# Queries of two heads by seven products of parts instead of eight, in the two 32-head attentions of a four-layer decoder kernel

## The reference, cut to what matters

```python
q = (query @ wq).reshape(bs, sq, 32, 128).transpose(0, 2, 1, 3)
k = repeat(key @ wk, 4 heads of queries to a head of keys)
v = repeat(value @ wv, the same way)
q, k = rope(q), rope(k)            # x * cos + rotate_half(x) * sin
attn = softmax(q @ k.T / sqrt(128) + mask)
x = layernorm(x + (attn @ v) @ wo)
```

## Time and profile before

| | us |
|---|---|
| median of 3 runs (lowest, highest) | 2778.18 (2775.37, 2780.76) |
| the profiled execution, its own time | 2781.93 |
| its span, first to last instruction | 2780.6 |
| stage 1, first key product to last output product, about | 169 to 862 |
| stage 4, the same | 1146 to 1837 |

### The profile page before, as it was taken

One profiled execution on the slowest core, in us unless ns is written; L12 is line 12 of the kernel. 1 busy time (PEld: TensorE's weight loads), 2 busy tenths in 40 slices (PEclk: granted clock), 3 DMA queues, 4 the chain that ended last, 5 costly groups with the idle time before them and its releaser, 6 DMA issues.

```text
span 2780.6 us, 40315 instructions
## 1 busy us (share of the span) xinstructions
PE 2649.1 (95%) x15720; PEld 1751.7 (63%) x15720; DVE 1640.8 (59%) x3081; ACT 851.6 (31%) x2630; POOL 458.8 (17%) x511
## 2 busy tenths in 40 slices
PE   8989999999999799899999999999998899999998
PEld 7855666666655566556666666556774455666664
DVE  3556667666666555466676666654555644344455
ACT  0012232222233355222222222323444412333331
POOL 1022212222202100122122222122211121000002
PEclk9999999999999999999999999999999999999999
DMA  8530001110000100001001000010000010000000
GB/s 182 92 128 25 37 38 39 38 38 16 16 1 38 69 2 2 27 23 39 38 38 39 37 18 6 11 69 31 2 2 28 21 63 27 15 27 1 12 1 31
DMA packets 53819, 94.86 MB, mean 34 GB/s; under 512 B 29408, under 2 KB 38560, under 8 KB 47488
## 3 DMA queue, kind: packets, MB, share of 16 engines
q1 hardware_dynamic: 53632, 92.30, 10.6%
HBM read 83.89 MB, written 8.39 MB: 33 GB/s over the span
## 4 chain that ended last, share of the span: by engine, by line
PE 88%; DVE 7%; ACT 3%; issue 1%; POOL 0%; DMA 0%; DVEq 0%; SPq 0%; POOLq 0%; ACTq 0%
PE banks L628 19%; PE banks L666 12%; PE banks L620 4%; PE banks L687 4%; PE banks L303 3%; PE banks L710 3%; PE banks L1210 3%; PE banks L650 3%; PE banks L1720 3%; PE banks L1772 3%; PE banks L2010 2%; PE banks L2042 2%; PE banks L1749 2%; PE banks L2075 2%; PE banks L1725 2%; PE banks L697 2%
## 5 line engine op out<-in xcount | busy, mean ns | idle before, releaser
L628 PE MATMUL banks<-xT,weights 128*128 128x512 f32 x1024 | 458.2, 592 | 0.0
L748 ACT ACTIVATE E_x<-S_x,sm_x 128x128 f32<-128x128 f32 x512 | 199.3, 390 | 586.7 <-DVE sm_x L838 586.7
L628 PEld LDWEIGHTS banks<-xT,weights 128*128 128x128 f32 x1024 | 188.9, 190 | 209.5 <-issue 206.6
L888 POOL TENSOR_TENSOR QT<-QT,turned 128x512 f32<-128x512 f32 x128 | 162.4, 1268 | 708.1 <-DVE QT L781 506.4
L779 DVE TENSOR_TENSOR turned<-banks,const 64x512 f32<-64x512 f32 x160 | 109.5, 684 | 234.1 <-PE banks L628 233.6
L809 DVE TENSOR_TENSOR x<-banks,x 128x256 f32<-128x256 f32 (+1 forms) x312 | 159.1, 510 | 123.2 <-PE banks L666 117.6
L161 POOL TENSOR_TENSOR norm_spread<-norm_mv,const 128x1 f32<-128x1 f32 x96 | 20.9, 218 | 1205.0 <-DVE norm_mv L157 1205.0
L666 PE MATMUL banks<-weights 128*128 128x256 f32 x832 | 206.9, 381 | 0.0
L666 PEld LDWEIGHTS banks<-weights 128*128 128x128 f32 x832 | 151.8, 190 | 39.6 <-DVE x L809 12.1
L666 PE MATMUL banks<-weights,OT 128*128 128x256 f32 x624 | 165.1, 387 | 12.1 <-DVE x L809 10.8
L2138 ACT ACTIVATE E_s<-banks,top_s 128x128 f32<-128x128 f32 x512 | 139.3, 383 | 62.9 <-DVE top_s L2235 62.9
(11 more groups left out here) (294 smaller groups left out, 4578.0 us busy)
## 6 DMA issues: line engine op xcount, KB each, us to landing
weights<-in_L_xwq SPq DMA_DIRECT2D x16, 1024.0 KB, 4.8
weights<-in_L_xwo SPq DMA_DIRECT2D x16, 1024.0 KB, 7.3
weights<-in_L_xwk SPq DMA_DIRECT2D x16, 256.0 KB, 5.1
weights<-in_L_xwv SPq DMA_DIRECT2D x16, 256.0 KB, 5.4
weights<-in_L_ffn_W_base SPq DMA_DIRECT2D x3, 1024.0 KB, 4.9
weights<-in_L_xwq SPq DMA_DIRECT2D x4, 768.0 KB, 5.0
weights<-in_L_xwo SPq DMA_DIRECT2D x4, 768.0 KB, 5.7
xT<-in_xT SPq DMA_DIRECT2D x4, 512.0 KB, 9.8
```

What stands on the lines that cost most here:

```text
L628: mm = PE.matmul(bank[:, :], weight, source[:, k, half_of(i)], start=k == 0, stop=k == KC - 1)
L748: ins = AC.activation(e[:, j, :], s[:, j, :], ACT.Exp, bias=sm[:, 0, j:j + 1], scale=1.0, accum_out=sm[:, 1, j:j + 1])
L888: PO.tensor_tensor(dst, dst, turned[j % 2][:, :, :], ALU.add).then_inc(*x_roped.one())
```

## The change

**Queries.** The 8 query jobs of a group become 6, three for each pair of heads `p`. The matrix of weights of two heads and the matrix of x in two halves of tokens are both cut in four parts, and the four blocks of queries (C11, C12, C21, C22) come out of the 7 products P1 to P7, each of 2 products of 128x128 by 512 columns: P2 and P1 in a pair's first job, P5, P6 and P3 in its second, P4 and P7 in its third. P1, P6 and P7 add up in one bank, the rest passes through the bank beside it. ACT copies a block's other term out of that bank into QT (`OTHER`), then DVE adds the first bank to it (`add_queries`); the next job waits for that add.

**Sums of parts.** POOL makes four sums of parts of wq for each group (`wq_sums`, each 128x512). DVE makes eight of x once a stage (`sums_of_xT`). `wo_sums` and `ot_sums` write one of their sums in place; `ot_sums` has four operations still, each now waiting for the one before.

**Rotation.** Of queries, DVE makes only the two sine products, now from QT in SBUF (`turn_queries`), placed in the steps by `shares` right behind the normalising. POOL makes the cosine product and the addition, two operations in place of one. Keys are as before.

**Order.** `plans` holds 10 jobs (b0 two of keys, b1 two of queries, b2 one, b3 two, b4 one, b5 and b6 one of values each, b7 none). In the opening the jobs of the two pairs alternate, values follow the queries in banks 3 and 4, and the second pair has banks 5 and 6. wq, wk and wv have one buffer each. 24 pairs of units in place of 26 go by parts, so that 16 units are plain. S has two buffers, not three. Three later attentions share semaphores with one another.

```diff
-                plans = [(1, 2, 2, 2, 1, 1, 1, 0)] + [(2, 2, 2, 2, 2, 1, 1, 0)] * (G8 - 2)
+                JOBS = (("k", 0), ("k", 1)) + tuple(("q", n) for n in range(6)) + (("v", 0), ("v", 1))
+                QUERIES = (tuple(("q", n) for n in (0, 3, 1, 4, 2, 5)),) + (JOBS[2:8],) * (G8 - 1)
+                ADDED = {0: ("C11",), 1: ("C12",), 2: ("C21", "C22")}
+                OTHER = {0: ("C11",), 1: ("C22", "C12"), 2: ("C21",)}
+                plans = [(1, 1, 1, 1, 1, 1, 1, 1)] + [(2, 2, 1, 2, 1, 1, 1, 0)] * (G8 - 2)
+                shares = [(0, 1, 1, 1, 1, 2, 1, 1)] + [(0, 1, 1, 2, 1, 1, 1, 1)] * (G8 - 2)
-                pairs = (units - B) // 2 - 2
+                pairs = (units - 2 * B) // 2
...
+                        if turn == 0:
+                            product("P2").then_inc(*x_other.one())
+                            product("P1").then_inc(*x_query.one())
+                        elif turn == 1:
+                            product("P5").then_inc(*x_other.one())
+                            product("P6")
+                            PE.wait_ge(*x_other_here(8 * g + place_of(g, p, "C22", OTHER) + 1))
+                            product("P3").then_inc(*x_other.one())
+                        else:
+                            product("P4").then_inc(*x_other.one())
+                            product("P7").then_inc(*x_query.one())
...
+                    def turn_queries(g, m):
+                        DV.wait_ge(*x_qadd(8 * g + m + 1))
+                        sines(NR * g + 2 + m, query(g, *blocks_of(g, ADDED)[m])).then_inc(*x_taken.one())
...
-                        DV.tensor_tensor(OS[:, 0], a21, a22, ALU.add)
-                        then(DV.tensor_tensor(OS[:, 2], a11, a21, ALU.subtract))
-                        then(DV.tensor_tensor(OS[:, 1], OS[:, 0], a11, ALU.subtract))
-                        DV.tensor_tensor(OS[:, 3], a12, OS[:, 1], ALU.subtract).then_inc(*x_ot_sums.one())
+                        then(DV.tensor_tensor(OS[:, 1], a11, a21, ALU.subtract))
+                        then(DV.tensor_tensor(a21, a21, a22, ALU.add))
+                        then(DV.tensor_tensor(OS[:, 0], a21, a11, ALU.subtract))
+                        DV.tensor_tensor(OS[:, 2], a12, OS[:, 0], ALU.subtract).then_inc(*x_ot_sums.one())
...
+                    def rope(j, to, cosines):
+                        PO.wait_ge(*x_taken(j + 1))
+                        if cosines:
+                            PO.tensor_tensor(four(to), four(to), spread(cos128, 4), ALU.mult).then_inc(*pool_step.one())
+                            PO.wait_ge(*pool_step.all())
+                        PO.tensor_tensor(four(to), four(to), turned[j % 2][:, :, :], ALU.add).then_inc(*x_roped.one())
...
+                    wq_sums(0)
                     for g in range(G8):
-                        for i in range(NJ):
-                            if g and i == 7:
+                        for i in range(2):
+                            rope(NR * g + i, KT[g % 2][:, half_of(i)], False)
+                        for m in range(8):
+                            if m == 2 and 1 <= g and 8 * (g - 1) < 2 * pairs:
                                 wo_sums(g - 1)
+                            rope(NR * g + 2 + m, query(g, *blocks_of(g, ADDED)[m]), True)
+                        if g + 1 < G8:
+                            wq_sums(g + 1)
```

More of the change, by code:

```diff
@@ L497, in load_cross, with place_rest, quarter @@
                 SP.dma_start(ctxT[:, :, :], dram["ctxT"]).then_inc(*ctx_in.one())
[L499 to L505, removed]
+            used = 3621 if stage == 4 else 2600
+            rest, taken = arenas[1 - stage % 2], [used]
+            def place_rest(n):
+                taken[0] += n
+                return rest[:, taken[0] - n:taken[0]]
+            def quarter(t, k):
+                return t.rearrange("p (k n) -> p k n", k=k)
+            views = {name: quarter(a.place(P, KC * n), KC) for name, n in (("wq", D), ("wk", P), ("wv", P))}
+            views["wq_sums"] = a.place(P, 3 * D).rearrange("p (s k n) -> p s k n", s=3, k=2)
+            views["wo"] = [quarter(t, 4) for t in (a.place(P, 4 * D), place_rest(4 * D))]
+            views["wo_sums"] = place_rest(3 * D).rearrange("p (s k n) -> p s k n", s=3, k=2)
+            views["ot_sums"] = place_rest(3 * D // 2).rearrange("p (s k n) -> p s k n", s=3, k=2)
+            for name, here in (("wk", xwk_in), ("wv", xwv_in), ("wq", xwq_in)):
+                SP.dma_start(views[name], dram[f"{layer}_x{name}"][0]).then_inc(*here.one())
             SP.dma_start(views["wo"][0], dram[f"{layer}_xwo"][0]).then_inc(*xwo_in[0].one())
@@ L508, in load_cross @@
                 views["mask"] = a.load("mask")
+            views["xT_sums"] = [a.place(P, D) for _ in range(3)] + [place_rest(D) for _ in range(2)]
+            assert taken[0] <= rest.shape[1]
             return layer, views, a.here.all()
@@ L512, in cross @@
             norm = Norm((0, 1))
-            wo, WS, OS = views["wo"], views["wo_sums"], views["ot_sums"]
+            wo, WS, OS, wq, QS = views["wo"], views["wo_sums"], views["ot_sums"], views["wq"], views["wq_sums"]
             units = B * G8
-            qkv_base, wo_base = [s.count - 48 for s in xwqkv_in], [xwo_in[0].count - 16, xwo_in[1].count]
+            wq_base, wk_base, wv_base = xwq_in.count - 16, xwk_in.count - 16, xwv_in.count - 16
+            wo_base = [xwo_in[0].count - 16, xwo_in[1].count]
             with ExitStack() as scope:
@@ L605, in pe_cross, with keys @@
                 def pe_cross():
-                    def job(g, i):
-                        bank = psum[i % 2]
+                    def keys(g, i):
                         if i == 0:
[L609 to L621, removed]
-                        else:
-                            source = ctxT if i < 2 else xT
-                            if g == 0 and i in (2, 3):
-                                PE.wait_ge(*before.here(4 * (i - 2) + 3))
@@ new lines, in keys @@
+                            PE.wait_ge(xwk_in.sem, wk_base + 16 * (g + 1))
+                        if g == 1:
+                            PE.wait_ge(*x_qadd(8))
+                        elif g:
+                            PE.wait_ge(*xv_here(2 * (g - 1) + i + 1))
+                        for k in range(KC):
+                            mm = PE.matmul(psum[i][:, :], views["wk"][:, k, :], ctxT[:, k, half_of(i)], start=k == 0, stop=k == KC - 1)
+                        mm.then_inc(*x_keys.one())
@@ L626, in job, with values @@
+                    def values(g, i):
+                        if i == 0:
+                            PE.wait_ge(xwv_in.sem, wv_base + 16 * (g + 1))
+                        bank = i
+                        if g:
+                            PE.wait_ge(*x_qadd(8 * g + 8))
+                        else:
+                            bank = 3 + i
+                        for b in range(4 * i, 4 * i + 4):
                             for k in range(KC):
-                                weight = views["wk"][g % 2][:, k, :] if i < 2 else views["wq"][g % 2][:, k, rows_of(head_of(i))]
@@ L631, in products, with job @@
+                    def job(g, kind, i):
+                        {"k": keys, "v": values, "q": queries}[kind](g, i)
                     def products(q, turn):
@@ new lines, in sums_of_xT @@
+                    def sums_of_xT():
+                        DV.wait_ge(*before.here(B - 1))
+                        b11, b12, b21, b22 = xT[:, 0:2, 0:HALF], xT[:, 0:2, HALF:T], xT[:, 2:4, 0:HALF], xT[:, 2:4, HALF:T]
+                        for k in range(2):
+                            then(DV.tensor_tensor(xT3[k], b22[:, k, :], b12[:, k, :], ALU.subtract))
+                            then(DV.tensor_tensor(b12[:, k, :], b12[:, k, :], b11[:, k, :], ALU.subtract))
+                            then(DV.tensor_tensor(xT2[k], b22[:, k, :], b12[:, k, :], ALU.subtract))
+                            ins = DV.tensor_tensor(xT4[k], b21[:, k, :], xT2[k], ALU.subtract)
+                        ins.then_inc(*xT_sums.one())
```

252 lines of the change are left out of this document (165 added, 87 removed).

## The result

The changed kernel takes 2852.7 us (median of 4 runs) against 2777.6 beside it: ratio 1.0269 (1.0251 to 1.0286). The direction was forecast, the size was not: 75 us where the sum gave 37, and the time lies above the range's 2840.

The account below looks back on a forecast made before the run. PE, busy 95% of the span, was taken as the bound. Savings and stalls summed to +18.3 us a stage, +36.6 for two, on 2781.93: 2818.5, or 2815 as the runs' median; range 2738 to 2840.

Parts of the forecast that it names:

- What PE saves: Query products: four fewer a group save PE 3.43 us, 54.9 in all; net of plain pairs, -51.6 us.
- DVE and POOL shut each other out: SBUF port: each waits for the other's whole instruction, in turns; a round takes 1.40 us, such a sum alone 0.42 to 0.46.
- the one at b4: b4, groups 1 to 5: PE waits 1.7 us for `ot_sums`, shut out by POOL's backlog; bounds 0 and 4.
- the port is kept: Rival: POOL does not split DVE's four sums; b0 costs 0.8 us, b4 0.5; 2765 us, chance 0.17.
- b0, the largest term: b0 of groups 1 to 6: PE waits 3.6 us for `ot_sums` alternating with POOL's wq_sums; 21.6 us a stage.
- b2 and b4 again: Steps with one part-0 job: PE waits 0.5 us for turn 0's add, ten or eleven times a stage.
- Group 0: Group 0: PE waits for copies behind exponentials, adds and probabilities; +6 us a stage, bounds 1 and 10.
- The opening: Start of a stage: waits for banks, sums of x and rotation give back the 3.43 us saved; +3, bounds 0 and 6.
- All hidden: Rival: all added work is hidden and PE's floor is reached, -45.6 us, 2733 us; chance 0.16.
- b0 alone: Rival: only b0 stalls beside the opening's cost, -1.2 us a stage, 2776 us; chance 0.15.

Follow-up runs that it names:

- e9: The changed kernel with the edits of e1, e5 and e7 together: 2757.7 us, 0.9926 of the kernel before.
- e1: The changed kernel with POOL's sums of wq moved behind the next group's first key block: 2788.8 us, 1.0042 of the kernel before.
- e5: On top of e1, one block of query sines in b3 and two in b4: 2771.6 us, 0.9976 of the kernel before.
- e8: The kernel before, with four dependent additions on POOL that nothing else uses, released at b0: 2824.3 us, 1.0166 of the kernel before.
- e2: The changed kernel with the second key product made once more on PE during b0's stall, 96 matmuls more: 2825.2 us, 1.0165 of the kernel before.
- e7: On top of e1, e4's earlier copies and, in group 0, one block of sines moved from b5 to b6: 2775.3 us, 0.999 of the kernel before.
- e4: The changed kernel with ACT copying block C22 before the exponentials in group 0: 2845.1 us, 1.0241 of the kernel before.

## Why the prediction was wrong in size

Stage 1, change of each part in us, forecast and measured:

| part | forecast | measured |
|---|---|---|
| opening | -0.4 | -1.8 |
| group 0 | +2.6 | +12.6 |
| groups 1 to 5, each | +2.8 | +3.6 to +5.8, mean 4.5 |
| group 6 | +2.3 | +4.0 |
| group 7 | 0 | +0.5 |
| whole | +18.3 | +37.8 |

Stage 4 came to +34.4, with +10.5 in group 0. The two are 72.2 of the 72.7 us by which the profiled executions differ.

- **What PE saves** held: two matmuls of 512 columns a product, 3.43 us a group. e9 shows part of it: 20 of 51.6 us.
- **DVE and POOL shut each other out** held in full, the port taken in turns included. The stall at b0 was 3.73 for 3.6 (2.92 in group 1), the one at b4 1.39 for 1.7. e1 and e5 take most of the first and all of the second away by moving POOL's or DVE's work, e8 makes the first anew. The rival "the port is kept" is out by L921 to L924 above, and by e8 even for sums that do not depend on each other.
- **b0, the largest term: the step that failed.** The prediction priced it by PE's idle time alone. The term of 21.6 us a stage put at nothing what PE may do after an idle time: it resumes at half clock. At b0 this added 1.4 to 3.0 us in eleven cases of twelve, 12.5 us in stage 1 and 10.7 in stage 4 (b0 against e2's, group by group), 23 of the 38 us that the forecast lacks. It was not among the rivals either, though the kernel before shows it at the start of stage 1: behind an idle time of 3.1 us, a clock of 0.95 in the opening's window, 0.50 in its first 2.8 us.
- **b2 and b4 again** was too dear: 0.2 us at b2 in place of 0.5. (For b4 the sum took 2.1 where its parts, 1.7 and 0.5, make 2.2.)
- **Group 0: the second step that failed**, +6 in place of +16 (12.6 and the 3.4 saved; +14 in stage 4), with bounds of 1 and 10. Its waits name the parts: the copy behind the exponentials, 3.2 us at b4 (2.0 in stage 4) where 0.9 was forecast, and 0.6 at b1 for 2.1; the probabilities, 3.5 for 4.3; DVE's sums at b6, 3.0, which was left out, since I stopped the hand schedule at b4; the second key block in front of the first query job, 1.4, left out too. The clock is 0.93 over the group: PE is busy 65.7 us where e7's, at a clock of 1.00, is busy 61.0, so an estimate of its share is 4.7 us. That part is chance as well: the same group 0 was 4.6 us shorter in stage 1 of e2. e4 and e7 show the copies and the block of sines as causes: 74.1 to 68.7 us.
- **The opening** cost 1.6 of the 3 that were allowed.
- **The rivals.** "All hidden" and "b0 alone" did not happen. e9 is nearer to what "hidden" described, which the change's own order did not reach.

The cause is settled for the main loop, but for one thing: what decides whether the clock falls behind a wait of 2 to 3 us stays open. Within group 0 the split between stalls and clock is an estimate: behind the same wait of 3.0 us at b6, step b6 took 14.2 us in group 0 of stage 1 in the changed kernel and 12.6 in e1.

## What to carry to other kernels

When work is moved to POOL, list which of DVE's operations with two SBUF inputs it will stand beside, and price each by a round of both engines, not by the load of either; then look for the PE instruction that waits behind them. An idle stretch of PE can cost more than its length, because the clock may fall behind it: 3.7 us of stall cost 1.6 to 3.0 us more here. Two executions of the same instructions can differ by such falls, so what an edit gave is read from the steps it touches, not from a group's time alone. And an order of instructions is part of a change: here the same operations are 2.7% slower or 0.7% faster than the kernel before.

## What the runs showed of the hardware

- PE given 96 matmuls more ran the kernel 27.5 us faster (e2). The Trainium skill ("TensorE: Matmul & The Clock Gate", section "Part 1: The HAM clock gate (the "warmup" mystery)") makes keeping TensorE's clock up a matter of its activity; this is that, as a measured trade.
- After idle times of 3.73 us (b0 of the changed kernel) the clock fell to half in ten cases of ten, after 2.05 to 2.15 us (b0 of e8) in eight of twelve, after 2.92 us (b0 of group 1) in one of two; after 1.39 us (b4) and 0.89 us (e1) it stayed at 1.00. After 2.95 us at b6 of group 0 the clock was 0.56 from 281.0 to 284.5 us in the changed kernel, and the eight matmuls behind it took 3.57 us; in e1, behind a wait of the same 2.95 us, it was 1.00 from 276 to 280 us, and they took 1.97. So the length of the idle time alone does not decide.
- Two operations of DVE that follow one another without a wait do not hold the port together: L790 ran 0.76 us and L791 1.26 with POOL's additions in between (e8).
